# A transformer layer on one core: both batches' fronts laid out in another order

## The reference, cut to what matters

```python
qg = hidden_states @ Wq;  q, gate = qg[..., :512], qg[..., 512:]
k, v = hidden_states @ Wk, hidden_states @ Wv
q, k = rope16(q), rope16(k)            # the first 16 of 64 dimensions are rotated
attn = softmax(q @ k.T / sqrt(64));  out = (attn @ v) * silu(gate)
x = layernorm(x + out @ Wo)
h = bitlinear(x, w_fc) + gate * (x @ v.T @ fast_b.T @ u.T)   # low rank, 16
r = maximum(h, 0)
x = layernorm(x + bitlinear(r * r, w_proj))
# bitlinear(x, w): w rounded to -1, 0, 1 by the mean of |w| of each row, times that mean
```

## Time and profile before

| | us |
|---|---|
| median of 3 runs | 1776.99 (1775.92 to 1777.12) |
| profiled execution: its own time | 1775.12 |
| profiled execution: span of the trace | 1773.3 |
| first projection, first pass, first exponential of batch 1 start at | 37.99, 60.36, 92.92 |
| last FFN matmul of batch 1 ends at | 895.4 |
| first projection, first pass, first exponential of batch 2 start at | 897.66, 925.75, 959.01 |

### The profile page before, as it was taken

How to read it: one execution, slowest core, us unless ns; L and a number is a source line. 1 busy time by engine, 2 the same in 40 slices (tenths; PEclk the granted TensorE clock), 3 DMA queues, 4 the chain that set the end, 5 groups by cost and what they waited for, 6 DMA issues and landing times.

```text
span 1773.3 us, 26408 instructions
## 1 busy us (share of the span) xinstructions
PE 1670.2 (94%) x6902; PEld 817.4 (46%) x6902; DVE 1390.5 (78%) x1692; ACT 742.0 (42%) x1407; POOL 989.9 (56%) x765
## 2 busy tenths in 40 slices
PE   5699999999999999999868999999999999999996
PEld 3444444444444444447744444444444444444585
DVE  6668888888888888757766788888888888885587
ACT  1244444444444444444422444444444444445352
POOL 0546666666666665653334566666666666657342
PEclk8799999999999999999987999999999999999998
DMA  4600101000000000020043010000000000000001
GB/s 163 159 18 23 23 23 24 22 22 22 23 22 22 22 20 19 1 78 24 25 115 84 18 29 23 23 23 22 22 22 23 22 22 22 19 1 1 25 25 48
DMA packets 36916, 59.76 MB, mean 34 GB/s; under 512 B 6624, under 2 KB 17264, under 8 KB 36288
## 3 DMA queue, kind: packets, MB, share of 16 engines
q1 hardware_dynamic: 36800, 58.50, 12.6%
HBM read 20.07 MB, written 4.19 MB: 14 GB/s over the span
## 4 chain that ended last, share of the span: by engine, by line
PE 75%; DVE 10%; issue 8%; ACT 2%; DMA 2%; POOL 1%; SPq 1%; DVEq 0%; ACTq 0%; POOLq 0%
PE ob L578 24%; PE trio L566 16%; PE trio L567 11%; PE sc L533 8%; PE trio L513 6%; PE trio L672 3%; DVE acc L328 2%; PE trio L589 2%; DVE maxp L1059 2%; PE sc L639 2%; ACT probs L824 2%; DMA acc<-in_x 1%; PE ob L687 1%; PE trio L687 1%; PE trio L525 1%
## 5 line engine op out<-in xcount | busy, mean ns | idle before, releaser
L328 POOL TENSOR_TENSOR acc<-acc,probs 128x512 f32<-128x512 f32 x448 | 577.2, 1288 | 435.1 <-DVE acc L328 377.2
L824 ACT ACTIVATE probs<-trio 128x512 f32<-128x512 f32 x1024 | 530.0, 603 | 654.5 <-PE trio L567 556.4
L1059 DVE TENSOR_REDUCE maxp<-sc 128x2 f32<-128x1024 f32 x472 | 575.1, 1218 | 138.6 <-PE sc L535 137.1
L578 PE MATMUL ob<-probs,v_sb 128*64 128x512 f32 x2048 | 495.8, 605 | 0.0
L328 DVE TENSOR_TENSOR acc<-acc,probs 128x512 f32<-128x512 f32 x448 | 429.9, 960 | 81.3 <-ACT probs L824 76.7
L566 PE MATMUL trio<-qa,kab 128*128 128x512 f32 x1024 | 459.8, 449 | 3.6 <-DMA qb<-mrow 3.6
L567 PE MATMUL trio<-qb,kab 128*128 128x512 f32 x1024 | 405.0, 396 | 0.0
L566 PEld LDWEIGHTS trio<-qa,kab 128*128 128x128 f32 x1024 | 192.4, 188 | 322.6 <-issue 210.7
L578 PEld LDWEIGHTS ob<-probs,v_sb 128*64 128x64 f32 x2048 | 123.9, 136 | 241.6 <-issue 178.8
L533 PE MATMUL sc<-kab,qa 64*128 64x512 f32 x512 | 197.1, 460 | 29.1 <-DVE maxp L1198 16.0
L567 PEld LDWEIGHTS trio<-qb,kab 128*128 128x128 f32 x1024 | 194.1, 190 | 23.4
(11 more groups left out here) (122 smaller groups left out, 1420.4 us busy)
## 6 DMA issues: line engine op xcount, KB each, us to landing
qa<-high_sb SPq DMA_DIRECT2D x128, 128.0 KB, 2.3
qb<-low_sb SPq DMA_DIRECT2D x64, 128.0 KB, 2.3
tables_sb<-in_tables SPq DMA_DIRECT2D x34, 128.0 KB, 2.4
xT_sb<-in_xT SPq DMA_DIRECT2D x2, 2048.0 KB, 10.2
acc<-in_x SPq DMA_DIRECT2D x8, 512.0 KB, 4.2
out_y<-acc SPq DMA_DIRECT2D x8, 512.0 KB, 3.1
kab<-acc SPq DMA_DIRECT2D x24, 128.0 KB, 2.4
rot_sb<-raw_sb SPq DMA_DIRECT2D x72, 32.0 KB, 1.8
```

Of the source, the lines that this page charges most:

```text
L328: ops.tensor_tensor(total, total, part, ALU.add).then_inc(summed, 1)
L578: mm = nc.tensor.matmul(ob[hd * D:(hd + 1) * D, :], v_sb[:, t, kv * D:(kv + 1) * D], probs[:, t % RING, hd * CHUNK:(hd + 1) * CHUNK], star ...
L824: nc.scalar.activation(probs[:, t % RING, hd * CHUNK:(hd + 1) * CHUNK], score_bank(t, hd), ACT.Exp, scale=float(D) ** -0.5).then_inc(probs ...
L1059: nc.vector.tensor_reduce(two_columns(p, j), MAX_PAIRS[j % 2], AX_X, ALU.max).then_inc(maxed, 1)
```

## The change

The change lays out both fronts anew.

- The stages come in the order k of chunk 0, q of pair 0, then as before. All rotations and all `low` instructions of the fronts run on POOL, one stage after another.
- The loads are reordered. `wk` and the first quarter of the first batch's tokens come first, then `w_fc` and the first 128 columns of `wq`. The other quarters follow from SP; the small FFN inputs, `w_proj`, `wv` and `wo` are issued from ACT.
- The FFN weights are prepared between the stages: the low-rank product after the second projection, transposes after the fourth projection and between passes, with their ACT copies put between the stage copies and roundings.
- Of a stage's six placing DMAs, two are made *early*: ACT issues them right behind the rounding, and a pass waits for those alone (semaphore `early`). The other four follow from SP when `low` is done (`placed`); the first score matmul of a unit waits for those.
- v is computed in half groups between pairs of passes. The last projection (stage 6) comes behind all passes and all v.
- In batch 2 the first two projections stand in the FFN of batch 1's last chunk, ahead of its last two `ffn_down` tiles, with their copies ahead of the last layer norm.
- The loop over the batches is written out, so counts outside of the inner loops are constants.

Its core:

```diff
-        FRONT = [("q", 0, 0, "dve"), ("k", 0, 1, "dve"), ("k", 1, 2, "pool"), ("k", 2, 3, "pool"),
-                 ("k", 3, 0, "pool"), ("q", 1, 1, "pool"), ("q", 2, 0, "pool")]
+        FRONT = [("k", 0, 0), ("q", 0, 1), ("k", 1, 2), ("k", 2, 3), ("k", 3, 0), ("q", 1, 1), ("q", 2, 0)]
...
+        def k_early(n):
+            keys = slice(n * CHUNK, (n + 1) * CHUNK)
+            return [(high, 0, ka[0:D, 0, keys]), (high, 0, kb[D:P, 0, keys])]
...
+        def place_early(eng, stage, b, targets):
+
+            slot = stage[0]
+            eng.wait_ge(rounded[slot], done(uses(stage, b) + 1))
+            for part, hd, dst in targets:
+                eng.dma_start(raw_words(dst), raw_words(part[slot][hd * D:(hd + 1) * D])).then_inc(early[slot], 16)
...
+            def front_begin(b):
+
+                if b == 0:
+                    sp.wait_ge(rot_cleared, 1)
+                else:
+
+                    sp.wait_ge(x1_done, done(b * NCH * TILES))
+                    sp.wait_ge(res_done, done(b * NCH * TILES))
+                front_tables(2, b)
+                front_swap(0, b)
+                front_swap(1, b)
...
+                front_tables(6, b)
+                front_swap(6, b)
+                sp.wait_ge(ones_set, 3)
                 place_max(b, 0, 0)
+                front_rest(5, b)
+                front_rest(6, b)
...
+                    if c == NCH - 1 and b < BATCH - 1:
+                        front_project(0, b + 1)
+                        front_project(1, b + 1)
                     ffn_down(first_n + c, range(JT - 2, JT))
...
+            def front_round(s, b):
+
+                what, n = FRONT[s][0:2]
+                if b >= 1 and s == 1:
+                    act.wait_ge(ffn2_ready, done(2 * b * NCH))
+                if b >= 1 and s == 2:
+                    act.wait_ge(res_done, done(b * NCH * TILES))
+                if s == 3:
+                    act.wait_ge(y_stored, 16 * (NCH * b + 1))
+                round_stage(front(s), b)
+                place_early(act, front(s), b, k_early(n) if what == "k" else q_early(n))
...
+            for b in range(BATCH):
+                front_rope(0, b)
+                if b >= 1:
+                    pool.wait_ge(y2_summed, done(b * NCH))
+                    nc.gpsimd.memset(probs[:, 3, :], 0.0).then_inc(late_cleared, 1)
+                front_rope(1, b)
+                front_rope(2, b)
+                front_low(0, b)
...
```

More of the change, by code:

```diff
@@ L510, in project, with setup_scale_row @@
+            def setup_scale_row():
+                pe.wait_ge(q_copied, done(5))
+                for i in range(2):
+                    mm = nc.tensor.matmul(FRONT_BANKS[4][i * D:(i + 1) * D, 0:HID], ones[:, :], wp_scale[:, :],
+                                          start=True, stop=True)
+                mm.then_inc(setup_pe, 1)
             def project(w, col, chunk, semaphore, bank):
@@ L541, in row_max @@
                 if j == 0 and not first(c, p):
-                    stage = behind(p - AHEAD, c)
-                    pe.wait_ge(placed[stage[0]], placed_before(stage, b, 1))
+                    stage = unit_stage(c, p)
+                    pe.wait_ge(early[stage[0]], early_before(stage, b, 1))
                 pe.wait_ge(maxed, done(unit * PASSES + j - 1))
@@ L724, in _, with front_maxima @@
-                v_group(0, b)
-                v_group(1, b)
+                def front_maxima(i):
+                    if i == 0:
+                        pe.wait_ge(early[1], early_before(front(1), b, 1))
+                    if i % TILES == 0:
+                        stage = front([f[0:2] for f in FRONT].index(("k", i // TILES)))
+                        pe.wait_ge(early[stage[0]], early_before(stage, b, 1))
+                    front_pair(0, i)
+                    front_pair(0, i + 1)
                 front_maxima(0)
-                v_group(2, b)
@@ L740, in _ @@
                     front_pair(1, i)
+                if b == 0:
+                    v_half(5, b)
+                    v_half(6, b)
+                v_half(7, b)
+                front_project(6, b)
+                for slot in range(SLOTS):
+                    stage = front([0, 1, 2, 3][slot]) if slot else front(4)
+                    pe.wait_ge(placed[slot], placed_before(stage, b, 1))
+                pe.wait_ge(ones_set, 3)
+                pe.wait_ge(q_copied, done(b * STAGES + PRO))
                 pe.wait_ge(v_copied, done((b + 1) * TILES))
@@ L781, in _ @@
-            for q in range(4):
-                nc.scalar.copy(wpT[:, 2 * q:2 * q + 2, :], sc[:, q, :].rearrange("p (a c) -> p a c", a=2))
-            last = nc.scalar.copy(wp_scale[:, :], misc[:, 0:HID])
-            last.then_inc(setup_act, 1)
-            def copy_stage(stage, number, b, in_front=False):
+            act.dma_start(fbT_sb, fast_bT).then_inc(small_loaded, 16)
+            for dst, src in ((v_lr_sb, v_lr), (gate_sb[:, :], gate), (uT_sb, uT), (ident[:, :], ident_in)):
+                act.dma_start(dst, src).then_inc(small_loaded, 16)
@@ new lines, in setup_wfc_copies, with setup_wp_copies @@
+            def setup_wfc_copies():
+                act.wait_ge(setup_pe, 3)
+                for h in range(HC):
+                    for q in range(2):
+                        last = nc.scalar.copy(wfcT[:, h, q * CHUNK:(q + 1) * CHUNK], sc[:, 2 * h + q, :])
+                last.then_inc(setup_act, 1)
+            def setup_wp_copies(half):
+                act.wait_ge(setup_pe, 4 + half)
+                for q in range(2):
+                    j = 4 * half + 2 * q
+                    last = nc.scalar.copy(wpT[:, j:j + 2, :], V_BANKS[q].rearrange("p (a c) -> p a c", a=2))
+                last.then_inc(setup_act, 1)
```

426 lines of the change are left out of this document (252 added, 174 removed).

## The result

The changed kernel takes 1795.9 us (median of 4 runs, 1791.3 to 1798.3) against 1777.05 before: ratio 1.0108, interval 1.0095 to 1.012. That is 18.9 us slower, where 3.5 to 4 us slower was forecast; the range ended at 1792. The profiled execution was the fastest of the four, 1791.34, which is 16.2 us above the one of before, and the comparison of the two traces goes against this number.

A forecast was written before the change was run, and what follows sets the result against it. PE, busy 1670.2 of 1773.3 us, bounds the kernel; only the fronts can move. Batch 1 -3.5, batch 2 +9.7, advance work -1.2, constant counts -1.5 make +3.5 us: 1781 after adjusting to the median, range 1764 to 1792.

The forecast's parts named there:

- side terms: Outside the fronts: constant counts in LN, FFN and 64 of 256 attention cycles save 1.5 us (0 to 6).
- the table load: ACT, batch 2: a load of 1.28 us moves from the front's head to the first exponential.
- First exponential of batch 1: Batch 1's front: first pass at 37.7, copy 6 at 78.5, first exponential at 89.4, 3.5 us gained.
- the first turn: A turn, per key chunk: passes, v halves, v's copy, rounding, issues, landing, 10 to 11 us; batch 1's pass 4 about 47.
- Early projections: Two batch 2 projections ahead of the last FFN tiles cost 3.6 us; first rotation done before the FFN's closing sum.
- From the first pass of batch 2 to the exponential: Batch 2's front: first pass at 911.4, then turns of 10 to 11 us, first exponential at 968.7.
- Issues from ACT: Each early DMA issued by ACT in the fronts costs 0.6 us, within bounds of 0.1 and 0.60.
- the rival with 0.1: ACT's early DMA issues cost 0.1 us each, so a turn loses 1.0; a condition within a rival of chance 0.25.
- the one of short turns: Between first pass and unit 1, turns take some 8 us, with cheap issues and PE's upper clock: 1766; chance 0.25.
- the landings of 4: Early DMAs land in 4 us under contention; four turns add another 6 us in batch 2, 1787.
- PE's first work done in advance: Scores precede the exponential's turn in each front: 0.6 us each, 1.2 together (0 to 1.8) saved.
- First pass of batch 2 not brought forward: Batch 2's first pass stays at about 920, turns move 9 us later: 1790; chance 0.12.

The follow-up runs named there:

- e1: Changed kernel with 64 more wait instructions, fulfilled at once, at the start of PE's list: 1780.7 us, ratio to before 1.0024.
- e2: Kernel before with only the loop over the batches written out: 1765.3 us (median of 10), ratio 0.9956.
- e8: e1 with the first two projections of batch 2 put back behind the last FFN tiles: 1779.1 us against 1780.7.
- e9: e1 with, on ACT only, key roundings and early transfers of chunks 1 and 2 ahead of FFN weight and v copies: 1767.6 us.
- e10: e1 with only stage 6 moved: its projection after pass 13, its copy before the last copies of v: 1759.6 us.
- e4: Changed kernel with attention's loop over the chunks written out as well: 1746.5 us, ratio 0.9831.
- e6: Kernel before with both loops written out, over the batches and over attention's chunks, fronts unchanged: 1724.4 us, ratio 0.9708.

## Why the prediction was wrong

The failed step is the one on side terms: "With the loop over the batches written out, counts are constants in LN, FFN and 64 of 256 attention cycles", and "I take -1.5 (0 to -6, by 0.1 in each of those cycles at most)". It was taken for a saving of counts alone. The runs show three things in its place. The counts saved more, 3.8 us in attention of batch 1 (e1 against before) and 3.8 in batch 2 (after against before), nearly all in the last 24 cycles. Without the batch loop, of whose head I carried only the table load, the front of batch 2 is 6.7 us shorter (e2), 4.2 of it ahead of ACT's first copy. And PE's list was laid out anew, which put 13.1 us of gaps at two jumps (after against e1). The first is a little beyond its bound of 6, the other two are in no term and no rival; the last is what took the time out of the range.

With the gaps away, e1 stands at 1780.7 and 4.5 us above the kernel before on the same chip, where I had 1781 and +3.5. That is luck, because its terms erred in both directions. In the trace of e1 batch 1 has 3.1 us more than forecast (-0.4 instead of -3.5), batch 2 has 4.3 more (+14.0 from FFN and front together instead of +9.7), and attention has 4.6 less (-7.3 instead of -2.7):

- *First exponential of batch 1*: -3.5 forecast, -0.55 measured. The first pass came at 40.2 instead of 37.7, since the swap landed late and POOL lost 1.9 us beside DVE instead of 1.0; in e1 it came at 37.7 and the exponential no earlier (92.5). Copy 6 at 83.4 instead of 78.5 is the term that failed, and the miss is all in the first turn: pass 4 came at 51.2 (51.95 in e1) instead of 47, because the rounding of its keys stood behind the weight copies until 46.81. From there the spacing was about as forecast. The 2.0 for contention was not there: from copy 6 to the exponential it took 8.94, without contention 8.9.
- *Early projections*: 3.6 forecast, 4.0 measured. The working has the first rotation done before the FFN's sum because of them, and puts the first pass 14 us earlier; they bring 2.4 of that (e8).
- *From the first pass of batch 2 to the exponential*: 57.3 forecast (968.7 - 911.4), 56.1 measured (58.2 in e1). The roundings stand 10.7, 10.7, 8.2 and 7.6 apart, where a turn was to be 10 to 11. e9 and e10 show the mechanism, each by taking away its part.
- *Issues from ACT*: 0.6 taken, 0.56 measured (1.12 for two); the rival with 0.1 is out, and so is the one of short turns, whose other condition failed as well: the granted clock was 0.68 from 923 to 979 us. In batch 2 the early DMAs landed in 2.6 to 2.8 us (medians by tile), so the landings of 4 that would have made 1787 did not come.
- *PE's first work done in advance*: 1.2 taken; no run shows it. From the first exponential to that of the eighth cycle it took 36.8 and 37.2 us in e1, and 36.1 and 36.5 before.
- *First pass of batch 2 not brought forward*: out. In the trace it is 2.2 earlier in spite of an FFN that ends 13 later, and 15 in e1.
- *The table load*: 1.28 at the second exponential, as taken. The 1.31 of idle that its row shows is the two issues, which end at 978.15, and the exponential follows at once. In e2 the load stands 0.01 behind a rounding. So the 2.86 of idle ahead of the load before was not part of a switch. The Trainium skill, "ScalarE: Activation LUTs", What ACT_TABLE_LOAD costs, has 2.66 with a drain; this place shows no more than 1.45 (978.15 to 979.61), and the drain is not seen.
- *Against which kernel*: the forecast set the new fronts against fronts slowed by the loop head. With the loops alike (e4 against e6) the new fronts lose 22 us, not the 5.0 of -3.5 + 9.7 - 1.2; what the written-out loop gave hid the rest.

## What to carry to other kernels

Changing loop structure is a change of its own, to be priced apart from the reordering that comes with it: here it was worth -8 to -11 us by itself, -51 together with the inner loop (e6), and +13 where an unlucky place of the code gave part of it back. A step that issues early must stand early on its engine: look at what is ahead of each rounding and each last stage in that list, since a queue in order turns any copy there into a wait for what the copy waits for.

## What the runs showed of the hardware

PE's attention loop could jump back in no visible time, or with 4.9 us of idle and a lower granted clock (0.88 and 0.80 in stretches of 14 and 17 us), by where it lay in PE's list: 32 or 64 instructions more ahead of it took the gaps away. With the gaps, instruction packets ran on q8 through the loop's second pass (6 from 310 to 460 us); where the same loop ran without gaps there were none. e4, which runs each instruction once there, moved 4 over that time without a gap.

In loops with computed counts a cycle of attention took 5.4 us, and 0.19 less written out, on a PE that reads as 99% busy. By the rows 0.155 of it stands ahead of ACT's first exponential of the cycle, which came 0.59 us behind the start of its score matmul instead of 0.43.

A DMA issue of 64x512 kept ACT for 0.56 us. POOL's elementwise instructions of 128x512 took 1.27 us, and 2.16 to 2.33 beside two DVE instructions of 128x1024.
